# Gated delta-rule layer on one core: the query/key projection of the plain steps in two halves further down TensorE's order, both output products together, the scans and VectorE's and GpSimd's shares moved

## What is computed

```python
qkvz = h @ W_qkvz                       # per key head: q 128, k 128, v 2x128, z 2x128
q, k, v = silu(causal_conv4(q, k, v))   # 4 taps along time
q, k = l2norm(q) * DK**-0.5, l2norm(k)
for t in range(T):                      # state S of 128x128 per value head
    S = S * alpha[t]
    S = S + outer(k[t], (v[t] - S^T k[t]) * beta[t])
    o[t] = S^T q[t]
og = o * silu(z)
og = og * rsqrt(mean(og*og) + eps) * norm_weight
x = x + gate * (og @ W_out)
```

## Time and profile before

| | |
|---|---|
| Time, median of 3 runs | 1450.24 us (1446.59 to 1454.74) |
| Profiled execution: its own time, its span | 1447.43 us, 1445.7 us |
| Busy share of PE, PEld, DVE, ACT, POOL | 83%, 68%, 65%, 56%, 49% |
| Mean granted clock of PE, of full | 0.924 |
| Blocks `kh` = 1 to 14 begin at | 221.2 us to 1042.3 us, 63.2 us apart |
| Blocks 7 and 8 begin at | 600.15 us, 664.11 us (block 9 at 726.98 us) |

### The profile page before, as it was taken

The page is one execution under the profiler, slowest core; times in us unless marked ns, Lnnn a source line. Parts: engine busy times, 40 slices in busy tenths (PEclk is TensorE's granted clock), DMA queues, the critical chain, the costliest instruction groups (busy, mean ns, idle before and its releaser), DMA issues. The chain is left out here.

```text
span 1445.7 us, 29726 instructions
## 1 busy us (share of the span) xinstructions
PE 1204.4 (83%) x10452; PEld 978.6 (68%) x10452; DVE 939.4 (65%) x2308; ACT 814.3 (56%) x2238; POOL 704.9 (49%) x1137
## 2 busy tenths in 40 slices
PE   4375799998999989899999989999987747978774
PEld 1255678887887878787788878878876633455453
DVE  2388577868777787787778677777823123134886
ACT  0333377677666667766776776666655323115871
POOL 0107576675857667585766758576663000010000
PEclk8578699999999999999999999999988676989997
DMA  3121303122230312123031222302102022000002
GB/s 119 56 64 50 97 7 98 31 72 41 64 98 13 93 31 72 39 67 98 8 97 32 72 42 63 98 7 62 31 18 58 1 76 72 0 1 1 2 2 91
DMA packets 141176, 73.84 MB, mean 51 GB/s; under 512 B 114612, under 2 KB 130500, under 8 KB 138980
## 3 DMA queue, kind: packets, MB, share of 16 engines
q1 hardware_dynamic: 141028, 71.94, 19.3%
HBM read 58.11 MB, written 13.78 MB: 50 GB/s over the span
## 5 line engine op out<-in xcount | busy, mean ns | idle before, releaser
L897 POOL TENSOR_TENSOR tmp<-Dm,Tn 64x31 f32<-64x31 f32 (+15 forms) x496 | 256.0, 516 | 98.0 <-DMA Dm<-blk_in_scratch 62.7
L900 POOL TENSOR_TENSOR Tn<-Tn,tmp 64x31 f32<-64x31 f32 (+15 forms) x496 | 284.5, 574 | 38.9
L742 DVE SCALAR_TENSOR_TENSOR cv<-bank,cw,cv 128x255 f32<-128x255 f32 (+2 forms) x384 | 155.3, 473 | 87.2 <-ACT cv L593 87.2
L873 POOL TENSOR_TENSOR ro<-ss,mhalf 128x4 f32<-128x4 f32 x64 | 66.1, 1033 | 243.2 <-ACT junk L655 220.6
L521 PE MATMUL bank<-wo,OTs 128*128 128x256 f32 x512 | 149.8, 418 | 23.9 <-ACT OTs L685 23.6
L742 DVE SCALAR_TENSOR_TENSOR cqk<-bank,cw,cqk 128x255 f32<-128x255 f32 (+2 forms) x384 | 154.7, 470 | 7.3 <-ACT cqk L593 7.3
L805 DVE SCALAR_TENSOR_TENSOR BP<-bank,cj,E 128x512 f32<-128x512 f32 (+1 forms) x256 | 142.8, 611 | 2.3
L521 PEld LDWEIGHTS bank<-wo,OTs 128*128 128x128 f32 x512 | 91.7, 199 | 44.3 <-ACT OTs L685 33.9
L655 ACT ACTIVATE junk<-og 128x129 f32<-128x129 f32 x256 | 79.7, 311 | 54.0 <-issue 41.8
L809 DVE TENSOR_TENSOR R<-Vs,bank 128x256 f32<-128x256 f32 x64 | 26.9, 421 | 124.8 <-PE bank L487 124.1
L593 ACT ACTIVATE cqk<-bank,cw 128x256 f32<-128x256 f32 x128 | 53.6, 470 | 91.0 <-PE bank L377 91.0
(11 more groups left out here) (203 smaller groups left out, 3448.5 us busy)
## 6 DMA issues: line engine op xcount, KB each, us to landing
alb<-alpha_scratch SPq DMA_DIRECT2D x8, 1024.0 KB, 6.3
rvz<-in_L_attn_W_qkvz SPq DMA_DIRECT2D x16, 512.0 KB, 5.5
x<-alpha_scratch SPq DMA_DIRECT2D x8, 1024.0 KB, 6.2
rqk<-in_L_attn_W_qkvz SPq DMA_DIRECT2D x16, 256.0 KB, 2.6
wo<-in_L_attn_W_out SPq DMA_DIRECT2D x16, 256.0 KB, 5.9
blk_in_scratch<-BP SPq DMA_DIRECT2D x256, 16.0 KB, 1.5
tinv_scratch<-Tn SPq DMA_DIRECT2D x32, 128.0 KB, 2.1
tinv_t_scratch<-Tt SPq DMA_DIRECT2D x32, 128.0 KB, 2.2
```

Of the source, the lines that this page charges most:

```text
L742: nc.vector.scalar_tensor_tensor(d, bk[:, t * T:(t + 1) * T - s], cw[p][:, first + t, TAPS - 1 - s:TAPS - s], d, ALU.mult, ALU.add).then_i ...
L897: pool_step_done(nc.gpsimd.tensor_tensor(t, Dm[:, j, j + 1:BLK].unsqueeze(2).broadcast_to([SLOTS, r, c]), Tn[:, j, 0:c].unsqueeze(1).broad ...
L900: pool_step_done(nc.gpsimd.tensor_tensor(Tn[:, j + 1:BLK, 0:c], Tn[:, j + 1:BLK, 0:c], t, ALU.subtract), kh * NTS + 2 * j + 4)
```

## The change

Five edits, all in the first layer:

1. PE, plain steps: `pe_qk` 0 moves from behind the gram to behind `pe_v` 1, `pe_qk` 1 to behind `pe_o` 0.
2. PE, plain steps: `pe_o` 1 moves ahead of `pe_f` 0, so that the two output products `pe_f` stand together.
3. ACT, plain steps: `act_tap0` of q and k moves from ahead of `act_y` 0 to behind `act_ots`, ahead of `act_turn`.
4. DVE: the four scans of steps 1 and 2 move to the end of the step before (0 and 1), behind the splits. Those of steps 3 and 0 stay.
5. POOL: `SPLIT` becomes 8, 11 and 12 columns.

```diff
@@ pe_step @@
-                if qk:
+                if qk and merges(b):
                     pe_qk(*qk, 0)
                     pe_qk(*qk, 1)
...
                         pe_v(*vz, 1)
+                    if qk:
+                        pe_qk(*qk, 0)
                     pe_ot(*last, 2 * (now + 3))
                     pe_solve(kh, p, b, 2)
                     pe_o(kh, p, b, 0)
+                    if qk:
+                        pe_qk(*qk, 1)
+                    pe_o(kh, p, b, 1)
                     pe_f(*last, 0)
-                    pe_o(kh, p, b, 1)
                     pe_f(*last, 1)
@@ act_step @@
-                if qk:
+                if qk and merges(b):
                     act_tap0(*qk, "qk", bQK, cqk, 0)
...
                     act_ots(*last)
+                    if qk:
+                        act_tap0(*qk, "qk", bQK, cqk, 0)
                     if kh + 1 < NKH:
                         act_turn(kh + 1, b - 2)
@@ dve_step @@
+                def scans(g):
+                    for n in range(2 * R):
+                        dve_scan(*g, n)
...
                 if gram:
-                    for n in range(2 * R):
-                        dve_scan(*gram, n)
+                    if not merges((b - 1) % B):
+                        scans(gram)
...
                 splits(kh, p, b, dve_split_qk, dve_split_vz)
+                if merges(b) and beside(kh, p, b, LEAD_GRAM + 1):
+                    scans(beside(kh, p, b, LEAD_GRAM + 1))
...
-            SPLIT = ((0, 7), (7, 18), (18, BLK - 1), (BLK - 1, BLK - 1))
+            SPLIT = ((0, 8), (8, 19), (19, BLK - 1), (BLK - 1, BLK - 1))
```

## The result

The changed kernel takes 1464.69 us (median of 4 runs, 1462.99 to 1467.07), the kernel before beside it 1450.07: a ratio of 1.0108, interval 1.0086 to 1.0131. That is 14.6 us slower. The forecast was 3.8 us faster, 1446.4.

What follows compares the result with a forecast made beforehand. POOL's row of work, with 8.25 us from the last `ro` to the next block, was taken to set the period. Blocks gain 2.3 us, with the tail 3.8 us: 1446.4 us, range 1436 to 1468.

Steps and rivals of the forecast that it cites:

- What bounds the kernel: Blocks 1 to 13: POOL's row of work sets the period; its only slack is 14.8 us of waits for sums.
- The scans: DVE: four moved scans take 2.5 us; `og`, sums and `ro` come 0.8 us later, step 2 takes 13.0 us.
- (c): Step 2 doesn't get shorter, late sums hold `y` 0, column 18 holds `ro` 1: 1450 to 1458 us; chance 0.11.
- the sum: Block 8 takes 62.4 to 62.8 us (62.87 before); blocks gain 2.3 us, with the tail 3.8 us.
- The products together: PE: `o` 1 ahead of `f` 0 is worth 0 in blocks 1 to 13, 1.5 us in blocks 14 and 15.
- POOL's parts: Same 31 columns; one more ahead of `ro` 0 and `ro` 1 costs 1.23 and 1.39 us, free where POOL waited.
- the halves: PE, step 2: q/k projection in halves behind other work, step 12.3 us instead of 13.78 (-1.5).
- The later `act_turn`: ACT: `act_turn` begins 1.2 us later, counted as nothing; without cover up to 1.2 us per block.
- (b): Step 3: PE's wait for `ogn` becomes 1.9 to 2.2 us, each clock fall loses 6 us, four give 1470; chance 0.18.
- The tail: Blocks 14 and 15: four plain steps wait ahead of the gram; gain between 0 and 2.0 us, taken as 1.5.

Runs made afterwards that it cites:

- POOL nearly idle: Both kernels with each of POOL's column instructions on one element for each partition: changed kernel 1393.44 us, kernel before 1426.99 us.
- POOL's parts alone: Kernel before with only POOL's columns split 8, 11 and 12: 1446.3 us, ratio 0.9977.
- scans alone: Kernel before with only the four scans of steps 1 and 2 moved to the end of the step before: 1481.5 us, ratio 1.0243.
- halves alone: Kernel before with only the q/k projection in halves further down and its ACT taps behind `act_ots`: 1472.98 us, ratio 1.0177.
- without the parts: Kernel before with edits 1, 2 and 3, without 4 and 5: 1466.44 us, ratio 1.0119.
- scans divided: Changed kernel with the two long moved scans between `dve_acc` and `dve_r2` of merge steps, the two short ones behind the split: 1440.09 us, ratio 0.9939.

## Why the prediction was wrong

**What bounds the kernel: right, but by a thin margin.** POOL's row and the chain behind the last `ro` set the block. With POOL nearly idle step 3 of the kernel before takes 13.84 us instead of 14.1 to 15.1, and its blocks 62.6 instead of 63.2: half a microsecond behind POOL's row stands the next limit. In the changed kernel the same edit takes 4.1 us out of a block (60.3 instead of 64.4). Taking the taps out of the chain gains again: 61.4 us instead of 62.6 for a block, both with the scans in their old place.

**The scans: the step that failed.** "Four scans take 2.5 us", ending 1.0 us into step 2, with `og` 0.8 us late and at most 1.1. Measured: 3.5 us, with the split ahead of them 0.4 longer, so that they end 2.29 us into step 2 and `og` is 2.1 us late. The 2.5 were read from a place where POOL's part ended halfway through the scans and POOL then waited; the new place lies wholly beside full columns. I had priced this contact as a loss of POOL, 0.4 us, and not as one of DVE. POOL's side came out as forecast: its columns of step 1 ended 39.04 us into the block, where I had put `ro` 1 at 38.6 to 39.0. It was the sums that came later. The Trainium skill, page "SBUF — State Buffer", section "Who interferes with whom", has them lock each other out, whoever is first. By that rule both are stretched, and the trace agrees: 2.13 and 1.51 us beside the columns, 1.26 and 0.71 without. I cited it and took only POOL's side of it.

**From there the sum follows by the prediction's own steps.** `ro` of step 1 was put at 3.5 us into step 2 and is at 4.73, 1.2 later. `ogn` ends 7.05 us into step 2 and not 6.0, and the chain behind it takes 7.08 where 6.95 to 7.05 were allowed. So step 2 takes 14.13 and not 13.0, the wait at PE's second solve included (0.98 us), and step 1 0.55 more instead of 0.2, as PE waits 0.5 us for `ogn` there too. From the last `ro` on it is 0.13 us longer, for which I had allowed 0.1. The block comes to about 64.4 us against the 62.4 to 62.8 forecast. Thirteen blocks of some 1.3 us over before are 17 us, one fall of the clock in block 2 nearly 3, the part ahead of block 1 is -1.3 and the tail -2.4: 16 us, where the span is 15.5 longer. Of the rivals, (c) had the mechanism (late sums hold `y` 0 and `ro` 1) at half its size: 1458.

**The other edits: nearly right, but not separable.** The products together at nothing in the blocks, POOL's parts alone at nothing: the runs show both. For the halves I had step 2 at 12.3 us; alone they give 12.6 to 13.1, and the 13.1 us beside POOL's new parts agree with my 13.0 by luck, as said above. The later `act_turn` cost nothing: step 0 stays at 17.5 us. What no step of the prediction contained is that the halves and the parts have to go together. Alone, the halves cost 25 us, by rival (b), which I had tied to the whole change; there the wait ahead of L511 is 1.81 us and in step 3 no fall followed it. I had put the wait at 1.9 to 2.2 us, nearly right, and left the clock's answer open. Its price was too high for this place: I had counted 6 us for each fall, and in step 3 a fall cost at most 2.0. By my own 6 us a single fall, not two, would have outweighed the 3.8 us of gain. And a row was misread. The wait of 2.25 us ahead of L487 was not without a fall: PE waited once more, 1.42 us ahead of L511, and from 1155.3 us on the clock was at half (the kernel before):

```profile
1155.30:1158.70 3.40, 3.29 (x12) 2.64 (x11) 0.00 (x0) 0.87 (x2) 0.00 (x0) 0.50 0.00 0
```

**The tail** gained 2.4 us; 1.5 were forecast. No run here tells what of it is edit 2: of the two pairs with and without it, one has the longer tail with it (401.2 against 398.9 us), the other without (404.8 against 401.0).

## What to carry to other kernels

The duration of an instruction belongs to the place where it was read. Before moving VectorE work that reads two tensors in SBUF, as these scans and the split do, see what GpSimd does at the new place, and price the contact on both engines. And if an edit shortens the steps ahead of a late arrival, PE's wait for it grows and can cost the clock: price it together with the edit that brings the arrival forward, or test them together.

## What the runs showed of the hardware

- A scan of 128x256 takes 0.63 us and one of 128x128 0.36 beside a nearly idle POOL, and 1.1 and 0.8 us beside its tensor-tensor instructions (halves of the rows above).
- The length of PE's wait alone doesn't settle whether the clock falls to its 1.2 GHz level. In step 3, waits of 2.24 to 2.32 us were followed by a fall 5 times in 12 (scans alone), waits of 2.3 to 3.0 us 13 times in 13 (halves alone) and 12 times in 13 (without the parts, where one of 2.96 us passed), waits of 1.80 to 1.87 us 3 times in 8 (scans divided) and never in 12 in the changed kernel. In merge steps, waits of 1.16 and 1.25 us were followed by a fall once each, two others of 1.25 us weren't. What else has to come together stays open.
- The price of a fall differs as much: 5.4 us in a merge step (24.1 against 18.7 us behind the same wait), in step 3 1.3 to 2.0 us (without the parts, waits of 2.96 us), 1.6 (scans divided, waits of 1.8) and 0.3 to 0.5 (scans alone, waits of 2.3).
